# The experts' gelu in the last layer, batches 0 to 2: tanh on ScalarE with products on GpSimd instead of the gelu table

## The reference

```python
def _moe_mlp(x, gate_w, gate_b, w1, w2):          # x: 4 x 1024 x 128
    xf = x.reshape(b * n, d)
    logits = xf @ gate_w + gate_b                    # 8 experts
    one_hot = jax.nn.one_hot(jnp.argmax(logits, axis=-1), E, dtype=xf.dtype)
    h = jax.nn.gelu(jnp.einsum('td,edh->teh', xf, w1), approximate=True)   # hidden width 512
    y = jnp.einsum('teh,ehd->ted', h, w2)
    out = jnp.einsum('te,ted->td', one_hot, y)
    return out.reshape(b, n, d)
...
x = x + _msa(_layernorm(x, ln1_w, ln1_b), w_qkv, w_proj)
x = x + _moe_mlp(_layernorm(x, ln2_w, ln2_b), gate_w, gate_b, w1, w2)
```

## Time and profile before

| what | us |
|---|---|
| median of 3 runs | 2766.81 |
| lowest and highest run | 2759.80, 2767.98 |
| span of the profiled execution, first to last instruction | 2676.7 |
| median less span (launch and what lies around it) | 90.1 |
| PE busy | 2323.5 (87%) |
| DVE busy | 1899.1 (71%) |
| ACT busy | 1773.8 (66%) |
| POOL busy | 890.3 (33%) |

### The profile page before, as it was taken

The page is one execution under the profiler, slowest core; times in us unless marked ns, Lnnn a source line. Parts: engine busy times, 40 slices in busy tenths (PEclk is TensorE's granted clock), DMA queues, the critical chain, the costliest instruction groups (busy, mean ns, idle before and its releaser), DMA issues. The chain is left out here.

```text
span 2676.7 us, 44214 instructions
## 1 busy us (share of the span) xinstructions
PE 2323.5 (87%) x15891; PEld 902.8 (34%) x15970; DVE 1899.1 (71%) x3300; ACT 1773.8 (66%) x3759; POOL 890.3 (33%) x1317
## 2 busy tenths in 40 slices
PE   4789989888988998998999999988989988988954
PEld 3222223222322344454444444322223323422424
DVE  6779987878797567656566666787986687697520
ACT  4288877766766666555656656578877777777741
POOL 5450132363254337327415114032023223214124
PEclk7699999999999999999999999999999999999977
DMA  4241103212313421440332122112113312311314
GB/s 161 94 131 28 36 23 107 55 48 85 94 33 100 140 65 58 119 134 24 121 103 70 47 81 68 42 38 68 27 30 114 91 32 85 111 40 54 115 32 169
DMA packets 137888, 205.50 MB, mean 77 GB/s; under 512 B 21130, under 2 KB 104426, under 8 KB 137494
## 3 DMA queue, kind: packets, MB, share of 16 engines
q1 hardware_dynamic: 119238, 141.52, 18.0%
q0 software_dynamic: 17536, 59.58, 7.3%
q10 hardware_dynamic: 896, 1.56, 0.2%
HBM read 138.52 MB, written 60.54 MB: 74 GB/s over the span
## 5 line engine op out<-in xcount | busy, mean ns | idle before, releaser
L1311 ACT ACTIVATE PB<-bank 128x512 f32<-128x512 f32 (+3 forms) x2944 | 1438.0, 556 | 565.8 <-PE bank L999 294.9
L1499 DVE TENSOR_REDUCE small<-unit 128x1 f32<-128x1024 f32 x1024 | 1210.9, 1219 | 243.0 <-PE unit L1019 233.5
L1019 PE MATMUL unit<-RK 61*128 61x512 bf16 (+4 forms) x2762 | 871.0, 375 | 129.3 <-DVE small L1499 74.4
L1139 PE MATMUL bank<-PB,VP 128*32 128x512 f32 (+3 forms) x5888 | 756.1, 567 | 13.4 <-ACT PB L1311 7.8
L999 PE MATMUL bank<-RK 64*128 64x512 bf16 x2048 | 678.2, 387 | 73.6 <-ACT PB L1311 39.9
L1496 DVE CUSTOM_DVE_ANT_0 unit<-unit,maskb 128x640 f32<-128x640 f32 (+7 forms) x512 | 387.6, 770 | 245.7 <-PE unit L1019 228.9
L1019 PEld LDWEIGHTS unit<-RK 61*128 61x128 bf16 (+1 forms) x2816 | 211.4, 95 | 560.2 <-DVE small L1499 230.2
L999 PEld LDWEIGHTS bank<-RK 64*128 64x128 bf16 x2048 | 154.2, 94 | 506.0 <-ACT PB L1311 324.3
L995 PE MATMUL bank<-RK 128*128 128x256 bf16 (+2 forms) x960 | 275.4, 296 | 1.7 <-issue 0.5
L994 PE MATMUL bank<-RK 128*128 128x256 bf16 (+3 forms) x935 | 264.5, 294 | 12.1 <-ACT PB L1311 4.8
L1765 POOL CAST small<-small 128x8 bf16<-128x8 f32 x128 | 24.8, 194 | 621.1 <-DVE small L1499 572.8
(11 more groups left out here) (197 smaller groups left out, 1961.4 us busy)
## 6 DMA issues: line engine op xcount, KB each, us to landing
RK<-qk_parts SPq DMA_DIRECT2D x128, 192.0 KB
qk_parts<-SC SPq DMA_DIRECT2D x48, 384.0 KB, 2.6
RK<-rqk_parts SPq DMA_DIRECT2D x48, 384.0 KB
qk_parts<-SC SPq DMA_DIRECT2D x48, 256.0 KB, 3.0
RK<-qk_parts SPq DMA_DIRECT2D x128, 96.0 KB
XSB<-x_sorted SPq DMA_DIRECT2D x38, 192.0 KB, 4.7
y_sorted<-XSB SPq DMA_DIRECT2D x38, 192.0 KB, 2.1
qk_parts<-SC SPq DMA_DIRECT2D x48, 128.0 KB, 2.9
```

The source lines that it names most:

```text
L1019: p = e.matmul(unit[k // 2 - 2][:, c0:c1], slot(L, u, 0, 0, rows)[:, 128 * qt:128 * qt + 128], slot(L, u, 1, 0, rows)[:, c0:c1], start=Tru ...
L1139: p = e.matmul(bank[k][32 * j:32 * j + 32, c0:512], VP[:, 8 * (pr // 8) + kt, 9 * h:9 * h + 32], prob(L, t)[:, c0:512], start=(kt == 0), s ...
L1311: e.activation(prob(L, t)[:, c0:512], bank[k][:, c0:512], ACT.Exp, scale=LAYERS[L].scale).then_inc(bank_free[k], 1)
L1499: e.tensor_reduce(m, unit[k // 2 - 2][:, :], AX.X, ALU.max, negate=True).then_inc(bank_free[k], 1)
```

## The change

For the last layer's batches 0 to 2 (by_tanh) the gelu of a tile is made in four steps. ScalarE copies half the input, x = v/2, from PSUM to RK (L1373 of the new kernel) and frees the bank. GpSimd makes x*x, then 4*0.044715*x^2 + 1, then times x (gelu_in; L1843, L1845, L1847). ScalarE takes the tanh in place with scale 2*sqrt(2/pi) (L1388). GpSimd multiplies by x and adds x (gelu_out; L1854, L1856). Three halves x are kept in RK, whose first 4096 columns layer 2's attention does not use. Batch 3 keeps the gelu of the table. The planner has costs for the three new steps and emits gelu_in behind each up, then tanh and gelu_out of the three tiles, then the three downs. down now waits for gelu_out.

```diff
     "gate0": (("DVE", 1.6), ("ACT", 1.0)), "gate0_end": (("DVE", 1.7),), "gate1": (("DVE", 0.25),),
     "rank": (("PE", 0.9), ("DVE", 1.4)), "place": (("DVE", 1.1),), "whose": (("DVE", 1.1),),
     "scatter": (("POOL", 2.0), ("DMA", 3.5)), "wload": (("POOL", 1.0), ("DMA", 5.0)), "xload": (("SP", 0.7), ("DMA", 4.5)),
+    "gelu_in": (("POOL", 3.1),), "tanh": (("ACT", 0.6),), "gelu_out": (("POOL", 2.5),),
     "xturn": (("PE", 0.85), ("ACT", 0.7)), "up": (("PE", 1.1), ("ACT", 0.75)), "down": (("PE", 1.1), ("DVE", 0.3)),
     "ystore": (("SP", 0.7), ("DMA", 3.0)), "collect": (("POOL", 2.0), ("DMA", 4.0)), "add_moe": (("DVE", 2.6),),
     "store": (("DVE", 0.7), ("SP", 0.7)), "fetch": (("SP", 0.9), ("DMA", 3.0)),
...
                 yield max([here["turned", q]] + [here["w", j] for j in tiles])
                 for j in tiles:
                     up(j)
+                    here["in", j] = P.do("gelu_in", M, b, j, after=here["up", j])
                 for j in tiles:
-                    yield here["up", j]
+                    yield here["in", j]
+                    t = P.do("tanh", M, b, j, after=here["in", j])
+                    here["out", j] = P.do("gelu_out", M, b, j, after=t)
+                for j in tiles:
+                    yield here["out", j]
                     down(j)
                 while freed:
                     yield here["down", freed[0]]
...
                     filled(g, step_of["turned", "n2", v, 1].banks)
                 else:
                     g.wait_ge(stored, P.nth("store", v, 2 * v + 1))
+
+        def by_tanh(M, b):
+
+            return M == 1 and b < B - 1
+
+        def half_x(n):
+
+            return RK[:, 512 * (n % HTN):512 * (n % HTN) + 512]
 
         def sorted_t(M, b, j):
 
...
                     M, b, j = a
                     (k, n), = s.banks
                     nf, w = (2, 4)[M], step_of["wload", M, b, j]
-                    taken(g, step_of["up", M, b, j].banks)
+                    if by_tanh(M, b):
+                        g.wait_ge(gelu_out, P.nth("gelu_out", M, b, j))
+                    else:
+                        taken(g, step_of["up", M, b, j].banks)
                     g.wait_ge(bank_free[k], n - 1)
                     for f in range(nf):
                         p = e.matmul(bank[k][:, 0:128], HT[:, s.n % HTN, 128 * f:128 * f + 128], expert(w)[1][:, 128 * f:128 * f + 128],
...
                     (k, n), = s.banks
                     w = step_of["wload", M, b, j]
                     o = HT[:, s.n % HTN, :]
+                    if by_tanh(M, b):
+                        here = P.nth("gelu_in", M, b, j)
+                        if here > HTN:
+                            g.wait_ge(gelu_out, here - HTN)
+                        g.wait_ge(bank_full[k], n)
+                        e.activation(half_x(here), bank[k][:, :], ACT.Copy, scale=0.5).then_inc(bank_free[k], 1)
+                        continue
                     if s.n > HTN:
                         filled(g, downs[s.n - 1 - HTN].banks)
                     g.wait_ge(bank_full[k], n)
...
                         e.activation(o[:, 128:256], bank[k][:, 128:256], ACT.Relu, bias=expert(w)[2][:, 1:2]).then_inc(bank_free[k], 1)
                     else:
                         e.activation(o, bank[k][:, :], ACT.Gelu_apprx_tanh).then_inc(bank_free[k], 1)
+                elif kind == "tanh":
+                    M, b, j = a
+                    o = HT[:, step_of["up", M, b, j].n % HTN, :]
+                    g.wait_ge(gelu_in, s.n)
+                    e.activation(o, o, ACT.Tanh, scale=2.0 * math.sqrt(2.0 / math.pi)).then_inc(gelu_tanh, 1)
 
         def vector(e):
             g = Gate(e)
...
                         taken(g, downs[s.n - 1 - WXN].banks)
                     e.indirect_dma_start(weights(k)[:, 0:(642, 1024)[M]], None, ins["experts%d" % M],
                                          bass.IndirectOffsetOnAxis(WI[:, j:j + 1], 0)).then_inc(wloaded[k], 16)
+                elif kind == "gelu_in":
+                    M, b, j = a
+                    n = step_of["up", M, b, j].n
+                    x, o = half_x(s.n), HT[:, n % HTN, :]
+                    g.wait_ge(*tail)
+                    filled(g, downs[n - 1 - HTN].banks)
+                    taken(g, step_of["up", M, b, j].banks)
+                    tick(e.tensor_tensor(o, x, x, ALU.mult))
+                    behind()
+                    tick(e.tensor_scalar(o, o, 4.0 * 0.044715, 1.0, ALU.mult, ALU.add))
+                    behind()
+                    e.tensor_tensor(o, o, x, ALU.mult).then_inc(gelu_in, 1)
+                    tail = (gelu_in, s.n)
+                elif kind == "gelu_out":
+                    M, b, j = a
+                    x, o = half_x(s.n), HT[:, step_of["up", M, b, j].n % HTN, :]
+                    g.wait_ge(*tail)
+                    g.wait_ge(gelu_tanh, P.nth("tanh", M, b, j))
+                    tick(e.tensor_tensor(o, o, x, ALU.mult))
+                    behind()
+                    e.tensor_tensor(o, o, x, ALU.add).then_inc(gelu_out, 1)
+                    tail = (gelu_out, s.n)
                 elif kind == "collect":
                     M, b, i = a
                     g.wait_ge(*tail)
```

More of the change, by code:

```diff
@@ L1 @@
+import math
 from collections import namedtuple
@@ L784, in build @@
         folded, rope_w = sem("folded"), sem("rope_w")
+        gelu_in, gelu_tanh, gelu_out = sem("gelu_in"), sem("gelu_tanh"), sem("gelu_out")
         qk_cut, rope_cut, rope_x, rope_hi = sem("qk_cut"), sem("rope_cut"), sem("rope_x"), sem("rope_hi")
```

## The result

| | median us | runs |
|---|---|---|
| before, on the chip of this comparison | 2764.8 | 2759.8 to 2768.0 |
| after | 2832.7 | 2829.8 to 2836.0 |

The ratio is 1.0245 [1.0224, 1.0265]: slower by 67.8 us. The forecast was 2820 us, from 2786 to 2862.

A forecast was written before the change was run, and what follows sets the result against it. PE was taken to bound stretches with experts and DVE's maxima those without; +12 (period), +20 (stall), +29 (end) and -7 (moved group) gave +54 on 2766.8, about 2820 us, range 2786 to 2862.

The forecast's parts named there:

- Instructions: Layer 2's experts: 30 table loads go, two stay; POOL products 1.16 us, tensor_scalar 0.7, ACT's tanh 0.60; 5.6 us on POOL per tile.
- Rival A: POOL's tensor_scalar in gelu_in is slow: at 3.2 us each the kernel takes 2932 us, at 1.6 us 2860; chance 15%.
- The period of a group, +12 us: Layer 2's attention: 15 score steps and a group take 27 us, before 26.1; PE waits for POOL, +0.9 for 14 groups.
- The loads: Among layer 2's experts: 30 table loads of 1.283 us; their time cost bounded by PE's idle 11.4 us, from above by 38.5.
- Rivals C: ACT sets the pace among the experts, so 28 removed loads give -36 us in place of +12: 2773 us; chance 6%.
- D: Each table switch costs 2.66 us, a 1380 ns drain beside its load, so removal gives 2732 us, faster than before; chance 2%.
- The stall, +20 us: At batch 2's first spread PE stands 19 us net behind batch 0's collects and layer norm, plus 1 to 2 at half clock; 14 to 26.
- The end, +29 us: Batch 2's fifth group stands behind the last attention, so proj_out ends 40.9 us after os instead of 12.0; 24 to 36.
- The group that left attention, -7 us: Batch 2's fifth group, moved behind the last os, no longer lengthens layer 2's attention: -7.2 us.
- The base: The 54 us were added to the median 2766.8 us, 90.1 above the profiled span of 2676.7; nothing outside the span was to change.

The follow-up runs named there:

- kernel 9: The change with the planner told that gelu_in, tanh and gelu_out cost 0.0, so groups stand almost at their old places; 2915.9 us, 1.0563 of the kernel before.
- kernel 11: The change, unchanged, rerun in the last comparison on a slower chip; 2829.9 us against 2766.3 before, ratio 1.0252.
- kernel 12: The change's order without POOL's products and separate tanh, tanh of the plain input in batches 0 to 2, slower chip; 2783.2 us, 1.0069 of the kernel before.
- kernel 2: The kernel before with Tanh in place of gelu in layer 2's batches 0 to 2, removing 30 table loads; 2662.7 against 2674.6 us, ratio 0.9967.
- kernel 3: The change's order with the table's gelu, its loads kept, no products or separate tanh; faster chip, 2736.8 us, 1.0229 of the kernel before.
- 4: The change's order without products, tanh of the plain input in batches 0 to 2, so two loads; faster chip, 2701.0 us, 1.0102 of the kernel before.
- kernel 6: The change for batch 2 alone, batches 0 and 1 keeping the table's gelu; 2792.0 against 2770.4 us before, ratio 1.0075.
- kernel 7: The change for batches 0 and 1 only, batch 2 keeping the table's gelu; 2802.7 against 2770.4 us before, ratio 1.0127.
- kernel 10: The change with planner costs 2.0, 0.5 and 1.6 for 3.1, 0.6 and 2.5, a group every 12 steps; 2851.6 us, 1.0309 of the kernel before.
- kernels 1 to 4: The comparison on the faster chip: kernel before unchanged, table loads alone removed, and the change's order without products, with and without loads; before takes 2674.6 us.
- kernel 8: The change with its products as three instructions on VectorE instead of five on GpSimd, planner costs 1.5, 0.65, 0.75; 2812.3 us, 1.0153 of the kernel before.
- kernel 1: The kernel before, unchanged, profiled again on the faster chip; 2676.4 against 2674.6 us, ratio 1.0006.

## Why the prediction was right, and where its sizes were off

The forecast, slower through waits for POOL and through the moved groups, held, and the time is inside the range. Step by step:

- **Instructions.** Two loads left: as said. Products 1.27 us, not 1.16; tensor_scalar 0.62, not 0.7; tanh 0.65, not 0.60. Together POOL has 5.5 us a tile (1.27 x 3 + 1.04 + 0.62), and 17.5/3 = 5.8 with the gaps, for the forecast 5.6. Rival A (a slow tensor_scalar, 15%) fell: the price by the form with constants led near, the one with column operands (four times 0.80) did not. The Trainium skill, "GPSIMD Engine Reference", section "Performance versus the Vector engine", has 1.03 cycles an element, from which the prediction estimated 0.64 us; the trace agrees with 0.62.
- **The period of a group, +12 us.** This is the term that was too small. The 27 us are what POOL needs (26.95 in kernel 9), but the forecast was for the change, whose periods are 29.6 us in the mean (kernel 11). The prediction's own addition falls short by a little: from the start of the second down at 13.4 us, two downs of 1.2 and 7 steps of 1.26 end at 24.6, not 24. Kernel 11 less kernel 12, products and tanh in one order on one chip, is 47 us by the medians and 39 by the spans (2825.6, 2786.5). About 16 of it lies behind the last os: proj_out ends there 43.8 us after os in the change, and in kernel 12, by the chain below, 28.1. That leaves 23 to 31 in attention, where the periods above show 28. Set against the loads' 9, it is +14 to +22 for the forecast +12. The forecast had one period of 15 steps, with PE waiting for POOL alone; in the trace PE also waits for weights and, longer than in kernel 12, for exps. On ACT exps stand in order behind tanhs, and ACT waits 8.2 us for POOL before these (row of L1388 above).

```profile
2661.59 0.61 ACT OS L1335
...
2689.07 1.21 DVE Z L1562 x2
```

- **The loads.** Priced at 0 to 11.4 by PE's idle time, up to 38.5 if all counted. Alone they are 9 to 12 us (kernel 2), as forecast, but in part by luck: 16 us were gained in attention, above the bound, and a fall of the clock took 11.6 back. In the new order they would cost 36 (kernel 3 less 4), but the change has none of them. Rivals C and D are out for the order that was: with 30 loads worth 9 to 16 us, most of their 38.5 was not on the path, let alone 41 us of drain. The Trainium skill, "ScalarE: Activation LUTs", section "What ACT_TABLE_LOAD costs", puts about 1380 ns of drain beside each; no run here shows it.
- **The stall, +20 us.** 18.2 us of PE's idle time for a forecast 19, and half clock for 10 us of work behind it, longer than forecast. Kernels 3, 4 and 12 have it too: it is the order's, not the products', as the prediction had it (collects and layer norm).
- **The end, +29 us.** Proj_out ends 43.8 us behind os, forecast 40.9, before 12.0: +31.8. POOL's part, forecast 16.8 (9.6 + 7.2), is 17.5; from the end of os to the first product it is 6.9 for 5.3, and the rest of the 3 us lies around the collects. Of the 31.8, 16.1 are there without any product (kernel 12), from the group standing behind the last attention; 15.7 come with the products.
- **The group that left attention, -7 us.** No run isolates it.
- **The base.** The forecast put 54 us on the median of 2766.8 and read the 90.1 us above the span as something outside it. They are the distance to another chip's profile. It did no harm, as the 54 us were added to runs of the right chip.

The terms as measured: order with the loads' gain +17 on a slower chip (+26 on the faster one), products and tanh +47, together 64 for a forecast of 54. About 3 of the 10 us missing are in the end; the others are by difference in the waits of attention. The split by batches supports the places: kernel 6 (late group only) +21.6, kernel 7 (stall only) +32.4.

None of the orders tried beats the kernel before. The planner's costs as changed were the best of the three with products on POOL: fewer steps in a period only make PE wait for POOL's 27 us (kernel 9 has 27.7 a period in batch 0 with 8 steps, kernel 10 still 28.9 with 12, over its three batches), and 15 groups at 15 steps do not fit into three batches of attention, which is why one is pushed behind its end and another up to the next spread.

## What to carry to other kernels

An engine at 33% busy is not free if its new work lies in series with a chain that is reused: what counts is the time from the first product to the buffer's release and reload (here 17.5 us of products, then 9.5 of load, landing and ups), set against the work that the others have in that period. That is only the least: even where the others' work was longer than POOL's 27 us, the order made PE wait at down, 2.4 us a period more than without products. The busy time of a removed thing is not its price: 38.5 us of table loads on an engine with slack were worth 9 to 12 us in one order and 36 in another, the clock included. The idle time of the bounding engine (11.4 us) came near in the first and told nothing of the second, so price it in the order that will run. And where a planner orders the work, a longer step moves its neighbours too; look for the place where its group no longer fits, and price that as a term of its own.

## What the runs showed of the hardware that was not expected

- Chips differ by 3.4% or more on the same program (before: 2674.6 us on one, 2766.3 and 2770.4 on two others), and nearly all of it lies in the span. The granted clock of these runs is 0.95 to 0.97 on the first and 0.94 to 0.95 on the others. The traces of the slower ones show idle times that end with no releaser in the profile, which the waits call "remote" (kernel after, ACT and DVE; the two rows of largest sum):

```profile
ACT PB L1330 <- remote: 48.4, 37, 5.4
DVE small L1530 <- remote: 41.2, 21, 4.5
```

  The traces of kernels 1 to 4, on the faster chip, have no such row, and the profile ahead of the prediction has one of 12.8 us. What it is stays open.
- A product on POOL of 128x512 float32 takes 1.04 us with one tile read twice and 1.27 with two; on DVE it takes 0.69 (kernel 8).
- After the 18 us pause PE's clock stayed at 0.50 for 10 us of busy work (windows above), and in kernel 2 it fell from 1.00 to 0.50 with PE busy before and after (windows of kernel 2), where kernel 1 kept it at 1.00:

```profile
2490.00:2500.00 10.00, 10.00 (x81) 6.36 (x80) 4.85 (x7) 5.19 (x10) 1.89 (x2) 1.00 0.11 39
...
2520.00:2530.00 10.00, 9.09 (x34) 1.27 (x35) 1.29 (x2) 6.42 (x13) 5.39 (x6) 0.50 0.17 46
```
